# Products with values of a whole diagonal as one unit, and pair weights folded ahead of the pair sum

## The reference

```
attn    = softmax(causal(q @ k.T * scale));  seq_out = attn @ v
inc     = read_lines . (write_lines @ J)          # 6 numbers per head and token
score_i = sum_{j<i} decay^(i-j) * inc_ij^2
gate    = mean_h sigmoid(score * mem_scale) * sigmoid(x @ memg_w + memg_b)
out     = (seq_out + gate * mem_val) @ out_w + out_b
```

## Time and profile before

| | us |
|---|---|
| median of 3 runs | 4106.52 (4101.76 to 4110.18) |
| the profiled execution | 4099.16 |
| its span, first to last instruction | 4096.4 |
| TensorE busy | 3843.2 (94%) |
| granted TensorE clock, mean | 0.969 |

### The profile page before, as it was taken

The page is one execution under the profiler, slowest core; times in us unless marked ns, Lnnn a source line. Parts: engine busy times, 40 slices in busy tenths (PEclk is TensorE's granted clock), DMA queues, the critical chain, the costliest instruction groups (busy, mean ns, idle before and its releaser), DMA issues.

```text
span 4096.4 us, 62172 instructions
## 1 busy us (share of the span) xinstructions
PE 3843.2 (94%) x19744; PEld 2326.3 (57%) x19744; DVE 3171.2 (77%) x6071; ACT 2653.7 (65%) x4142; POOL 2205.0 (54%) x1724
## 2 busy tenths in 40 slices
PE   7999999999999999997989999999999999999998
PEld 3656665656565655655545565555555555555554
DVE  3789999999999999999485766857667576685763
ACT  6777778777878878775246465565655546555454
POOL 4787998988999999998131312313132131321311
PEclk9999999999999999998989999999999999999999
DMA  4444554444555555555221122211222212221111
GB/s 156 134 138 162 164 164 154 151 153 160 165 163 169 159 168 159 156 163 183 83 71 56 48 72 56 87 56 59 67 58 79 56 57 66 61 80 56 56 46 27
DMA packets 251030, 442.10 MB, mean 108 GB/s; under 512 B 25860, under 2 KB 80596, under 8 KB 249812
## 3 DMA queue, kind: packets, MB, share of 16 engines
q1 hardware_dynamic: 250708, 438.14, 34.9%
HBM read 366.39 MB, written 69.21 MB: 106 GB/s over the span
## 4 chain that ended last, share of the span: by engine, by line
PE 54%; DVE 10%; ACT 6%; issue 6%; DMA 0%; POOL 0%; DVEq 0%; SPq 0%; ACTq 0%; POOLq 0%
PE ps L1403 7%; PE ps L1506 6%; PE ps L1514 6%; PE ps L1365 5%; PE ps L1384 5%; PE ps L1434 3%; PE ps L1267 3%; PE ps L1316 3%; DVE ps L1901 2%; PE ps L1440 2%; PE ps L1277 2%; DVE ps L1923 2%; PE ps L1487 1%; PE ps L1445 1%; ACT L1531 1%
## 5 line engine op out<-in xcount | busy, mean ns | idle before, releaser
L2146 POOL TENSOR_TENSOR drive<-du,b_wide 128x1024 f32<-128x1024 f32 x512 | 1201.8, 2362 | 200.1 <-DVE held L1901 116.0
L2181 POOL TENSOR_SCALAR_AFFINE_SELECT exps<-exps 128x256 f32<-128x256 f32 x512 | 217.6, 426 | 1373.0 <-ACT exps L1531 1372.2
L1531 ACT ACTIVATE exps<-ps 128x1024 f32<-128x1024 f32 (+3 forms) x768 | 620.9, 810 | 487.2 <-PE ps L1384 460.4
L1531 ACT ACTIVATE ps<-delta,neg_a 128x512 f32<-128x512 f32 x1024 | 682.0, 685 | 151.3 <-DVE heavy L1879 137.1
L1923 DVE CUSTOM_DVE_ANT_0 ps<-ps,later 128x128 f32<-128x128 f32 (+3 forms) x1024 | 483.6, 512 | 194.8 <-PE ps L1365 190.2
L1316 PE MATMUL ps<-p_all,heavy 128*128 128x128 f32 x3072 | 440.9, 280 | 71.4 <-DVE heavy L1879 64.0
L1316 PEld LDWEIGHTS ps<-p_all,heavy 128*128 128x128 f32 x3072 | 363.3, 144 | 241.5 <-DVE heavy L1879 117.7
L1879 DVE TENSOR_TENSOR heavy<-c_wide,ps 128x512 f32<-128x512 f32 x704 | 468.6, 671 | 8.1 <-issue 4.0
L1901 DVE TENSOR_TENSOR_SCAN ps<-ps,carry,drive 128x512 f32<-128x512 f32 x352 | 441.7, 1273 | 32.4 <-ACT ps L1531 32.1
L1901 DVE TENSOR_TENSOR_SCAN ps<-ps,drive 128x512 f32<-128x512 f32 x352 | 420.6, 1215 | 48.7 <-ACT ps L1531 46.9
L1926 DVE TENSOR_REDUCE smax<-ps 128x2 f32<-128x1024 f32 x256 | 312.4, 1220 | 116.4 <-PE ps L1365 113.8
(11 more groups left out here) (193 smaller groups left out, 6562.9 us busy)
## 6 DMA issues: line engine op xcount, KB each, us to landing
b_wide<-bc_dram SPq DMA_DIRECT2D x512, 256.0 KB, 3.4
c_wide<-bc_dram SPq DMA_DIRECT2D x512, 256.0 KB, 3.5
stacks<-parts SPq DMA_DIRECT2D x192, 256.0 KB, 2.4
qs<-stacks SPq DMA_DIRECT2D x128, 192.0 KB
ks<-stacks SPq DMA_DIRECT2D x128, 192.0 KB, 4.3
x_row<-in_x SPq DMA_DIRECT2D x14, 1024.0 KB, 7.9
resid<-mix SPq DMA_DIRECT2D x9, 1024.0 KB, 5.4
x_row<-resid SPq DMA_DIRECT2D x9, 1024.0 KB, 5.8
```

What stands on the lines that cost most here:

```text
L1531: return nc.scalar.activation(out_, in_, func, **kw)
L2146: G.tensor_tensor(drive[:, g % DRIVE_SLOTS, :, :], du[:, e, :, :], wide(b_wide[:, g % B_SLOTS, :], MD), ALU.mult).then_inc(driven, 1)
```

## The change

1. **Products with values.** A chunk's four diagonal key tiles become one unit of 8 matmuls, in the order 0, 1, 3, 2. The bands alternate by the place in that order, so 512 and 128 columns go to one pair of bands, 384 and 256 to the other. Units left of the diagonal stay pairs. A pair of heads has 4 product units in place of 6. The ring's `need`, the waits of `turn` and the planner follow.
2. **Pair weights.** VectorE makes, once at the start, `rates` = weight x decay for each feature row, and cuts `sumpq` to at most 1. The product (line 2040) takes `rates` in place of `rate`. Two new GpSimd tasks per half row (`sum`) add parts 1 and 2 of `prod` onto part 0, and `ms` makes one matmul per token tile in place of three.
3. **The planner.** `LAG` 5 for 3, other `SPANS`, a shorter length for `ms`.

```diff
+def out_tiles(jt, ch):
+    if jt // TC == ch:
+        return [TC * ch + i for i in (0, 1, 3, 2)] if jt % TC == TC - 1 else []
+    return [jt - 1, jt] if jt % 2 else []
...
-        need = max([n // 2 + 1 for n, (a, w, _) in enumerate(plan) if n >= len(plan) - 24 and a < at + width
+        need = max([OUT_OF[EXPS[n]] + 1 for n, (a, w, _) in enumerate(plan) if n >= len(plan) - 24 and a < at + width
...
-LENGTH = {"xt": 0.55, "qk": 1.8, "pa": 1.6, "pb": 1.35, "lt": 0.5, "jw": 0.6, "fw": 0.5, "fr": 0.5, "ms": 1.1,
+LENGTH = {"xt": 0.55, "qk": 1.8, "pa": 1.6, "pb": 1.35, "lt": 0.5, "jw": 0.6, "fw": 0.5, "fr": 0.5, "ms": 0.5,
-LAG = 3
-SPANS = {"early": (-46, -22), "late": (-24, 8), "second": (-4, 20), "mlp": (14, 86), "close": (8, 28)}
+LAG = 5
+SPANS = {"early": (-40, -30), "late": (-24, 8), "second": (-12, 24), "mlp": (20, 74), "close": (4, 30)}
...
+            for ch in range(1, FCH):
+                add("g", ("sum", b, c, ch), 1.27, place["fr", b, c, ch] + 1, ("v", "fr", b, c, ch))
             for i in range(2):
-                dense(("ms", b, c, i), ("v", "fr", b, c, FCH - 1))
+                dense(("ms", b, c, i), ("g", "sum", b, c, FCH - 1))
...
-                    if e[2] == 1 and g + ch:
+                    if e[2:] in ((TC - 1, 0), (1, 1)) and g + ch:
                         pe.wait_ge(oT_done, NC * g + ch)
-                    for parity in range(2):
-                        jt = e[2] - 1 + parity
+                    for place_of, jt in enumerate(out_tiles(e[2], ch)):
+                        parity = place_of % 2
...
-                    drained(pe, plan, ("fr", b, c, FCH - 1), "v")
+                    pe.wait_ge(prod_summed, (FCH - 1) * (NC * b + c + 1))
...
-                        for ch in range(FCH):
-                            last = mm(bank[:, j * H:(j + 1) * H], prod[:, ch, tt * P:(tt + 1) * P],
-                                      pick[0:FR, ch, :], start=(ch == 0), stop=(ch == FCH - 1))
+                        last = mm(bank[:, j * H:(j + 1) * H], prod[:, 0, tt * P:(tt + 1) * P], param("sumpq")[0:FR, 0:H],
+                                  start=True, stop=True)
...
+            link("v", V.tensor_reduce(times, param("sumpq")[0:FR, :].rearrange("p (c h) -> p c h", c=FCH), AX_X, ALU.max))
+            link("v", V.tensor_scalar(times, times, param("decay")[0:FR, :], None, ALU.mult))
+            V.tensor_scalar(param("sumpq")[0:FR, 0:H], param("sumpq")[0:FR, 0:H], 1.0, None, ALU.min).then_inc(setup_v, 1)
...
-                    V.scalar_tensor_tensor(prod[:, ch, :], gsum[:, ch, 0:HALF], rate, bank[0:FR, :], ALU.mult, ALU.mult)\
+                    V.scalar_tensor_tensor(prod[:, ch, :], gsum[:, ch, 0:HALF], rates[:, ch:ch + 1], bank[0:FR, :], ALU.mult,
+                                           ALU.mult)\
...
+                elif kind == "sum":
+                    c, ch = task[2:]
+                    drained(pool, plan, ("fr", n, c, ch), "v")
+                    if ch > 1:
+                        pool.wait_ge(prod_summed, (FCH - 1) * (NC * n + c) + ch - 1)
+                    G.tensor_tensor(prod[:, 0, :], prod[:, 0, :], prod[:, ch, :], ALU.add).then_inc(prod_summed, 1)
```

More of the change, by code:

```diff
@@ L395 @@
 EXPS = [(g, jt, ch) for g in range(PAIRS) for jt, ch in exp_chunks()]
+def out_tiles(jt, ch):
+    if jt // TC == ch:
+        return [TC * ch + i for i in (0, 1, 3, 2)] if jt % TC == TC - 1 else []
+    return [jt - 1, jt] if jt % 2 else []
+OUT_UNITS = [(jt, ch) for jt, ch in exp_chunks() if out_tiles(jt, ch)]
+OUTS = [(g, jt, ch) for g in range(PAIRS) for jt, ch in OUT_UNITS]
+OUT_OF = {(g, t, ch): n for n, (g, jt, ch) in enumerate(OUTS) for t in out_tiles(jt, ch)}
 def exps_plan():
@@ L456, in dense @@
         if kind in EMPTY_V:
-            add("v", unit, EMPTY_V[kind], place[unit], (("a" if kind == "qk" else "p"),) + unit, *v)
+            add("v", unit, EMPTY_V[kind], place[unit], (("a" if kind in ("qk", "pa", "pb") else "p"),) + unit, *v)
     def tiles(*kind):
@@ L488, in pair @@
             add("p", unit, SCORES[width], tick, ("s", "maxima", g))
-            add("a", unit, 0.17 + width / 602, tick, ("p",) + unit, ("p", "pv") + EXPS[2 * used - 1] if used else None)
+            add("a", unit, 0.17 + width / 602, tick, ("p",) + unit, ("p", "pv") + OUTS[used - 1] if used else None)
             last = ("a",) + unit
@@ L493, in pair @@
                 add("g", ("select",) + unit[1:], 0.41, tick, ("a",) + unit)
-            if jt % 2:
+            if out_tiles(jt, ch):
                 turned = ("a", "turn") + ((g, 0) if ch else (g - 1, NC - 1))
-                add("p", ("pv",) + unit[1:], 0.08 + (exp_width(jt - 1, ch) + width) / 1180, lag, ("a",) + unit, last,
-                    ("v", "pa", b, jt), turned if jt == 1 and g + ch else None)
+                add("p", ("pv",) + unit[1:], 0.08 + sum(exp_width(t, ch) for t in out_tiles(jt, ch)) / 1180, lag,
+                    ("a",) + unit, last, ("v", "pa", b, jt), turned if (jt, ch) in ((TC - 1, 0), (1, 1)) and g + ch else None)
             if jt == TC * (ch + 1) - 1:
@@ L688, in all_tasks @@
             ("s", "stack", 0): [("g", "clear", 3)], ("v", "sm", 0, 0, 0): [("a", "later"), ("g", "clear", 1)],
-            ("p", "pv", 0, 1, 0): [("g", "clear", 4)], ("v", "square", 0, 0): [("v", "o", last, TC - 1)],
+            ("p", "pv", 0, TC - 1, 0): [("g", "clear", 4)], ("v", "square", 0, 0): [("v", "o", last, TC - 1)],
             ("s", "resid", 0): [("s", "keep", B - 1)], ("v", "e1", 0, 0): [("s", "weights")],
@@ L940, in build @@
         gsum_set = sem("gsum_set")
+        prod_summed = sem("prod_summed")
         q_in = [sem(f"q_in{i}") for i in range(SLOTS)]
@@ L1310, in _ @@
             pe.wait_ge(params_more_in, 16)
+            pe.wait_ge(setup_v, 2)
             def add_y(j, e, u, d):
@@ L1468, in dense @@
                     c, i = unit[2:]
-                    drained(pe, plan, ("fr", b, c, FCH - 1), "v")
-                    pick = param("sumpq").rearrange("p (c h) -> p c h", c=FCH)
+                    pe.wait_ge(prod_summed, (FCH - 1) * (NC * b + c + 1))
                     for j in range(2):
                         tt = 2 * i + j
-                        for ch in range(FCH):
-                            last = mm(bank[:, j * H:(j + 1) * H], prod[:, ch, tt * P:(tt + 1) * P],
-                                      pick[0:FR, ch, :], start=(ch == 0), stop=(ch == FCH - 1))
+                        last = mm(bank[:, j * H:(j + 1) * H], prod[:, 0, tt * P:(tt + 1) * P], param("sumpq")[0:FR, 0:H],
+                                  start=True, stop=True)
                 elif kind == "zt":
@@ L1697, in attention_task @@
                     ch = task[2]
-                    act.wait_ge(pt_read, UNITS // 2 * n + (TC // 2 if ch == 0 else UNITS // 2))
+                    act.wait_ge(pt_read, len(OUT_UNITS) * n + (1 if ch == 0 else len(OUT_UNITS)))
                     if n and ch == 0:
@@ L1869, in _ @@
             dve.wait_ge(params_more_in, 16)
+            times = param("ew")[0:FR, 0:FCH]
+            dve.wait_ge(setup_v, 1)
+            link("v", V.tensor_reduce(times, param("sumpq")[0:FR, :].rearrange("p (c h) -> p c h", c=FCH), AX_X, ALU.max))
+            link("v", V.tensor_scalar(times, times, param("decay")[0:FR, :], None, ALU.mult))
+            V.tensor_scalar(param("sumpq")[0:FR, 0:H], param("sumpq")[0:FR, 0:H], 1.0, None, ALU.min).then_inc(setup_v, 1)
             def weigh(k):
@@ L1904, in _ @@
             plan = L1_PLAN
-            scale, rate = param("scale"), param("decay")[0:FR, :]
+            scale, rate, rates = param("scale"), param("decay")[0:FR, :], param("ew")[0:FR, 0:FCH]
             by_head = "p (h d) -> p h d"
```

## The result

The changed kernel takes 4015.49 us (median of 4 runs, 4006.38 to 4020.04) against 4105.06 for the kernel before (4 runs): ratio 0.9778, interval 0.9764 to 0.9793. That is 90 us faster. Against the profiled execution of before, 4099.16 us, the sum gave 4038; the profiled execution of after took 4020.04. So 18 us of the miss show in the profiles.

A forecast was written before the change was run, and what follows sets the result against it. TensorE's time in layer 1 was taken as the bound. The terms -43 (units) - 31 (folding) + 2 (additions) + 6 (order) + 5 (tail) = -61 us gave 4038 from the profiled 4099.16, about 4046 for the median; range 4022 to 4084.

The forecast's parts named there:

- What bounds the kernel: Layer 1, 2100 to 4030 us: TensorE is busy 97%, so an edit is worth the TensorE time it removes.
- The four-tile unit, 1.20 us, bands with queues of their own: Diagonal product units: 1.20 us in place of 1.53, each band running on by itself; 128 units save 43 us.
- The folded weights, 0.48 us: Sum over pairs: four records a unit in place of 12, 0.48 us for 1.44; 32 units save 31 us.
- Additions on GpSimd: Two additions per half row, 1.3 us each, 42 us in all on GpSimd; 2 us taken for TensorE's wait.
- The ring, 0: Ring of exponentials: columns wait for the whole diagonal unit, but two score units lie between; 0 in the dense stretch.
- The tail, 5 us: Kernel's end, last row: about a pair more (20 us) runs without filler, at 27% idle 5 us lost.
- The order, +6 given back: MLP's ticks 14 to 86 become 20 to 74, leaving less filler beside attention and the memory features: 6 us lost.
- Rival (c): New priorities and lag also remove some 25 us of layer 1's idle time and clock loss: 4021; chance 0.08.
- Rival (b): Where filler is missing the next engine bounds; half the gain returns as idle time or lower clock: 4074; chance 0.13.

The follow-up runs named there:

- band_major: The changed kernel with the same diagonal tiles on the same bands, but all of one pair of bands issued first (0, 3, 1, 2): 4019.9 us, ratio 0.9784.
- order_0123: The changed kernel with the diagonal tiles in plain order, so that the bands carry 768 and 512 columns: 4033.1 us, ratio 0.9817.
- hold_only: The kernel before, with only the ring columns of the diagonal's exponentials held until that diagonal's last product unit is done: 4115.2 us, ratio 1.0017.
- units_only: The changed kernel without the folded weights, at LAG 3 and the old SPANS: 4098.1 us, 0.9978 of the kernel before.
- units_new_plan: The changed kernel with weights unfolded and the pair sum in three matmuls again, LAG 5 and new SPANS kept: 4086.4 us, ratio 0.9938.
- mlp_old: The changed kernel with only the MLP's span put back to ticks 14 to 86: 4068.0 us, ratio 0.9899, clock 0.961.
- The six spans: The changed kernel with the MLP over ticks 20 to 74, 14 to 86, 14 to 74, 20 to 86, 20 to 70 or 24 to 68: 4016 to 4068 us.

## Why the prediction was right and wrong

- **What bounds the kernel** (TensorE's time in layer 1): right. In the profiled executions busy time fell by 83 us and the span by 78.
- **The four-tile unit, 1.20 us, bands with queues of their own:** right, 1.22 us; band_major and order_0123 show both halves of the reasoning. The value of a unit in the whole kernel was the 41 us only in the new order with folded weights.
- **The folded weights, 0.48 us:** right, 0.45 to 0.47. Wrong was to price them by TensorE's time alone. The earlier trace rows already showed 1.44 us for 12 records of 16 columns; I read it as a cost in time and not as thin work for the clock.
- **Additions on GpSimd:** right, 1.27 us and hidden: the sum over pairs waited for them twice, 1.3 us in all, for which the forecast took 2.
- **The ring, 0:** not refuted; hold_only is 5 to 7 us slower, without the wait that the argument was about. **The tail, 5 us:** TensorE's MLP ended 69 us ahead of the end before and 78 after (3940.1 of 4018.3). That is 9 us more without filler, not 20; at the last stretch's idle share of 30% it is under 3 us.
- **The order, +6 given back, and no term for the clock:** this step failed. It put a price on idle time and none on the clock, and took the spans for something with a slope. In the profiled pair the sum comes out term by term. The two edits saved 71 us by the lengths of their units (forecast 74). Idle time gave back 5 (forecast 2 + 6 + 5 = 13). And the time lost to the lower clock, half of the time at that level, fell from 125 to 113 us: 12 us more saved, where the forecast had 0. That is -71 - 12 + 5 = -78, the change of the span. Between the medians the clock is worth more. By time x clock the change is -63 (3972 to 3909), and the rise from 0.967 to 0.974 is worth some 24 to 30 us (at 3.4 us for each 0.001, or in proportion to the clock). Without the clock the profiled pair gives -71 + 5 = -66 where the sum has -61: near, with two misses that partly cancel.
- **The range** reached beyond the saved 74 us only by 10. Rival (c), with 0.08, named "part of the clock's 58 us", and its 4021 came nearest; but it also wanted less idle time, which didn't come.
- **Rival (b)** (less dense TensorE lowers the clock) happened in units_only, units_new_plan and mlp_old, at 15 to 50 us. (c) is the same thing with the other sign, and which of them comes out changed with the static order. The six spans go from 4016 to 4068 with a mean of 4044, 2 us from the forecast. They are six chosen spans and no random draw, but they say that a range of 62 us with nothing in it for the clock was too narrow, since the clock alone moves the time by 50 us.
- **Left open:** why LAG 3 and the old spans make the units and the folding collide in 38 us of idle time. The waits name exponentials (18.5 us) and many small ones; no run tells which of them comes first. That thin work causes falls of the clock is read from what precedes them in all the traces and from the higher clock of the folded kernel in all four pairs; no run changed the thinness of a matmul and nothing else. Of the 50 us between neighbouring orders the runs show that they are the clock, and not why one order has more falls than another.

## What to carry to other kernels

Price an edit of TensorE's work twice, by its time and by what it leaves beside it: where dense matmuls were taken out, the clock fell in three of four pairs and took back half of the saving in one; where thin ones were, it rose in all four, and in the final order the gain was twice their time. Where matmuls sit on separate bands of the array, sum the columns of each band, and balance them; of two issue orders on the same bands neither was faster. And where a static order is planned by constants, measure neighbours before crediting a constant: four ticks moved this kernel by 48 us at the same work.

## What the runs showed of the hardware

- Matmuls on different bands of the array start out of program order: a unit took 1.22 us with its bands interleaved and with one pair of bands issued wholly ahead of the other, and in the second case 384 columns started 0.85 us before 128 that were issued ahead of them.
- The granted clock fell to 0.50 right behind 3.4 us in which TensorE was busy for 3.40 us, most of it with matmuls of 16 moving columns. The Trainium skill ("TensorE: Matmul & The Clock Gate", What's actually happening) ties the clock to how busy TensorE has been; here the profile's busy time alone doesn't tell when the clock falls. In the twenty profiles 59 falls in layer 1 had TensorE idle for at most 0.3 of the 3.4 us ahead, all with thin matmuls there.
- 23 executions of one kernel differed by 29 us (4090.1 to 4119.6) along with their mean clock (0.971 to 0.963), 3.4 us for each 0.001.
